# Attention: queries and placed row maxima summed in PSUM by TensorE, and copied out by ScalarE

## The chip, the cores and the metric

One core of one Trainium2 chip runs the whole program in one launch. The number that counts is the device time of that launch in microseconds (us), as the median of several runs. TensorE (PE; PEld is its weight load), VectorE (DVE), ScalarE (ACT), GpSimd (POOL) and the queues of DMA each run their own instructions in order and meet at semaphores.

## What is computed

Four sublayers follow one another on a residual x of 2 x 512 tokens by 512 channels: causal attention with 32 heads of 16, a gated feed-forward with low-rank side weights, a mixer, and a gated feed-forward with quantized weights. The change is inside the attention:

```
q = (x @ wq).reshape(b, s, H, HD); k = (x @ wk).reshape(b, s, H, HD); v = ...
q = _apply_rotary(q, cos, sin);    k = _apply_rotary(k, cos, sin)
scores = jnp.einsum('bqhd,bkhd->bhqk', q, k) * scale
scores = jnp.where(causal[None, None], scores, jnp.finfo(scores.dtype).min)
probs = jax.nn.softmax(scores, axis=-1)
out = jnp.einsum('bhqk,bkhd->bqhd', probs, v).reshape(b, s, d) @ wo
```

## The kernel before

The attention handles 32 pairs of heads (a pair of heads of one batch entry; `PAIRS`). Queries and keys of a pair stand in `q_stack(g)` and `k_stack(g)`, parts of `xt_hi` and `xt_lo` of 128 partitions by 512 tokens: 64 partitions a head, three copies of 16 channels split into high and low parts, and two spare partitions for a row maximum. Each pair is done in two passes.

- ONE (four blocks i = 3, 2, 1, 0 of 128 queries): TensorE makes scores (L1264) and adds the causal mask with four small products (L1268); VectorE takes the negated row maxima (`negmax`, L916) and, after block 0, writes them as a high and a low part into `max_row` (L924, L925).
- PLACE: TensorE multiplies `max_row` by an identity, four products of 128 columns (L1294), so that the maxima land in bank 6 of PSUM on the two spare partitions, zeros elsewhere. VectorE adds `q_stack(g)` to it and writes the sum into `q_less_max(g)`, a part of `w_hi` (L929).
- TWO (four blocks): TensorE makes the transposed scores less their maxima from `k_stack` and `q_less_max` (L1302), ScalarE takes the exponential into `probs` (L743), GpSimd zeroes the upper triangle of the diagonal block (L649).
- PV (per two pairs, four blocks): probabilities by values, into bank 7 (L1313). ScalarE copies bank 7 out after block 3 (`heads_t`, L749), FLIP turns it on TensorE (L1287) and VectorE divides by the sums (L937, L938).
- TURN (every fourth pair): TensorE turns a block of queries and keys (L1222), ScalarE copies it out as a high part (L737), VectorE subtracts for the low part (L913). The queue of SP writes both to `turned` in HBM, and GpSimd's queue loads the next stacks from there (STACK, L630).

One list, `PERIODS`, sets the order for all engines; each engine picks its own entries from it and runs them in that order. A period handles TWO of pairs a and b, and ONE of the next two:

```
(TWO a 0) (ONE next_a 3) (TURN) (PLACE b) (TWO a 1) (ONE next_a 2) (PV m-1, 3) (TWO b 0) (ONE next_a 1) (TWO b 1)
(ONE next_a 0) (PV m, 0) (TWO a 2) (ONE next_b 3) (FLIP) (PV m, 1) (TWO b 2) (ONE next_b 2) (PLACE next_a) (TWO a 3)
(ONE next_b 1) (PV m, 2) (TWO b 3) (ONE next_b 0)
```

m counts the periods from 0 to 15, after an opening one (m = -1). TURN stands in the opening one and in m = 0, 2, 4, 6, 8, 10. ONE, TWO, TURN and FLIP share a ring of three pairs of PSUM banks in the order of the list: an entry of TensorE waits (`ring_free`) until the third one before it has been read. So in a period without TURN the first product of TWO b waits for the maxima of ONE next_a 3, in one with TURN for the low part of TURN (L913). Besides, TWO i = 0 of a pair waits for its `q_less_max`.

Of the kernel before, what the change touches and what calls it, by code (L numbers as in the profile page):

```python
# [14 lines left out]
F32 = mybir.dt.float32  # L15
# [3 lines left out]
ALU = mybir.AluOpType  # L19
# [3 lines left out]
P = 128  # L23
# [24 lines left out]
def sandwich(nc, a, out):  # L48
# [3 lines left out]
    def sem(name):  # L52
        if name not in sems:
            sems[name] = es.enter_context(nc.semaphore(name))
        return sems[name]
# [4 lines left out]
    with es:  # L60
# [640 lines left out]
        def _(act):  # L701
# [28 lines left out]
            for e in PERIODS:  # L730
                what, g, i = e
                if what == TURN:

                    act.wait_ge(sem("block_psum"), g + 1)
                    if g >= 3:
                        act.wait_ge(sem(f"turned_out{g % 2}"), 12 * 16 * (g // 2))
                    nc.scalar.activation(turned_hi(g), pair_of_banks(e), ACT.Copy).then_inc(sem("block_hi"), 1)  # L737
                elif what == TWO:
                    act.wait_ge(sem("scores_t"), nth[e] + 1)
                    if nth[e] >= PROBS:  # L740
                        _, g0, i0 = TWOS[nth[e] - PROBS]
                        act.wait_ge(sem("pv"), TB * (g0 // 2) + i0 + 1)
                    nc.scalar.activation(probs[:, nth[e] % PROBS, :, 0:(TB - i) * P], pair_of_banks(e)[:, :, 0:(TB - i) * P],  # L743
                                         ACT.Exp).then_inc(sem("exp"), 1)
                elif what == PV and i == TB - 1:
                    act.wait_ge(sem("pv"), TB * (g + 1))
                    if g >= 2:
                        act.wait_ge(sem("flipped"), g - 1)
                    nc.scalar.activation(heads_t[:, g % 2, :], bank[7][:, :], ACT.Copy).then_inc(sem("heads_t"), 1)  # L749
# [92 lines left out]
        def _(dve):  # L842
# [66 lines left out]
            for e in PERIODS:  # L909
                what, g, i = e  # L910
                if what == TURN:
                    dve.wait_ge(sem("block_hi"), g + 1)
                    nc.vector.tensor_tensor(turned_lo(g), pair_of_banks(e), turned_hi(g).bitcast(F32), ALU.subtract).then_inc(sem("block_split"), 1)  # L913
                elif what == ONE:
                    dve.wait_ge(sem("scores"), nth[e] + 1)
                    nc.vector.tensor_reduce(negmax[:, g, i, :], pair_of_banks(e)[:, :, 0:(i + 1) * P], AX_X, ALU.max,  # L916
                                            negate=True).then_inc(sem("row_max"), 1)
                    if i == 0:

                        dve.wait_ge(sem("row_max"), TB * (g + 1))  # L920
                        if g:
                            dve.wait_ge(sem("placed"), g)
                        rows = max_row[:, :, :].rearrange("p i (h r) -> p i h r", h=2)
                        link(nc.vector.tensor_copy(rows[:, :, :, 3 * HD], negmax[:, g, :, :]))  # L924
                        nc.vector.tensor_tensor(rows[:, :, :, 3 * HD + 1], negmax[:, g, :, :], rows[:, :, :, 3 * HD].bitcast(F32),  # L925
                                                ALU.subtract).then_inc(sem("max_row"), 1)
                elif what == PLACE:
                    dve.wait_ge(sem("placed"), g + 1)
                    nc.vector.tensor_tensor(q_less_max(g), bank[6][:, :], q_stack(g).bitcast(F32), ALU.add).then_inc(sem("q_less_max"), 1)  # L929
                elif what == FLIP:  # L930

                    b, n = divmod(g, NPAIR // 2)
                    dve.wait_ge(sem("flipped"), g + 1)
                    if b:
                        dve.wait_ge(sem("wo_split"), KD)
                    src = pair_of_banks(e)[:, 0, :].rearrange("p (i h r) -> p i h r", i=TB, h=4)
                    link(nc.vector.reciprocal(einv[:, g, :, :], src[:, :, :, HD]))  # L937
                    nc.vector.tensor_tensor(y[:, TB * b:TB * b + TB, 4 * HD * n:4 * HD * (n + 1)].rearrange("p i (h d) -> p i h d", h=4),  # L938
                                            src[:, :, :, 0:HD], einv[:, g, :, :].unsqueeze(3).to_broadcast([P, TB, 4, HD]),
                                            ALU.mult).then_inc(sem("o_ready"), 1)  # L940
# [260 lines left out]
        def _(pe):  # L1201
# [70 lines left out]
            for e in PERIODS:  # L1272
# [10 lines left out]
                elif what == FLIP:  # L1283
                    ring_free(e)
                    pe.wait_ge(sem("heads_t"), g + 1)
                    for t in range(TB):
                        ins = nc.tensor.transpose(pair_of_banks(e)[:, 0, t * P:(t + 1) * P], heads_t[:, g % 2, t * P:(t + 1) * P], ident[:, :])  # L1287
                    ins.then_inc(sem("flipped"), 1)
                elif what == PLACE:
                    pe.wait_ge(sem("max_row"), g + 1)  # L1290
                    if g:
                        pe.wait_ge(sem("q_less_max"), g)
                    for t in range(TB):
                        ins = nc.tensor.matmul(bank[6][:, t * P:(t + 1) * P], max_row[:, t, :], ident_r[:, :], start=True, stop=True)  # L1294
                    ins.then_inc(sem("placed"), 1)
                elif what == TWO:
                    ring_free(e)
                    if i == 0:
                        pe.wait_ge(sem("q_less_max"), g + 1)
                    for h in range(2):  # L1300
                        rows = slice(64 * h, 64 * h + 64)
                        ins = nc.tensor.matmul(pair_of_banks(e)[:, h, 0:(TB - i) * P], k_stack(g)[rows, i * P:(i + 1) * P],  # L1302
                                               q_less_max(g)[rows, i * P:S], start=True, stop=True)
                    ins.then_inc(sem("scores_t"), 1)
                elif what == PV:
                    pe.wait_ge(sem("probs"), nth[TWO, 2 * g + 1, i] + 1)
                    if i == 0 and g:
                        pe.wait_ge(sem("heads_t"), g)
                    for four in range(4):
                        pair, h = 2 * g + four // 2, four % 2  # L1310
                        b, p = PAIRS[pair]
                        col = (2 * p + h) * (HD + 1)
                        ins = nc.tensor.matmul(bank[7][32 * four:32 * four + 32, i * P:S], v[:, TB * b + i, col:col + 32],  # L1313
                                               probs[:, nth[TWO, pair, i] % PROBS, h, 0:(TB - i) * P], start=(i == 0), stop=(i == TB - 1))
                    ins.then_inc(sem("pv"), 1)
# [252 lines left out]
```

## Time and profile before

| what | value |
|---|---|
| runs | 897.25, 898.45, 899.44 us, median 898.45 |
| profiled execution | 898.1 us, of which the span is 896.0 |
| busy in the span | PE 770.9, DVE 557.7, POOL 433.4, ACT 316.8 us |
| attention with its pairs | about 107 to 326 us of the span: PE 188.0 of 219.0, DVE 152.16, ACT 103.01, POOL 67.31 |
| granted TensorE clock there | 0.87 of full, mean |

A granted clock of 1.00 is 2.4 GHz, 0.50 is 1.2 GHz; values between are means of stretches that hold both. The engines of the attention work one after another on each pair and in parallel on different pairs, so the busy shares alone don't say what one instruction is worth: that is read from the place where it stands in a period, and from what waits for it.

### The profile page before, as it was taken

How to read it: one execution, taken by the hardware profiler on the slowest of the kernel's cores; microseconds unless marked ns; L12 is line 12 of the kernel's file. 1: busy time of each engine (PE TensorE's matmuls, PEld its weight loads, DVE VectorE, ACT ScalarE, POOL GpSimd, SP SyncE). 2: the span in 40 equal slices, each digit the busy share in tenths (PEclk: the TensorE clock that was granted, in tenths of full speed). 3: DMA queues.
4: the chain of work that ended last, by engine and by line, in shares of the span. 5: the costliest groups of instructions: out<-in, count | busy, mean ns of one | idle time of the engine just before them, and what ended most of it. 6: DMA issues, size and time to landing. Idle time of an engine off the chain costs nothing.

```text
span 896.0 us, 12432 instructions
## 1 busy us (share of the span) xinstructions
PE 770.9 (86%) x4387; PEld 559.8 (62%) x4387; DVE 557.7 (62%) x1130; ACT 316.8 (35%) x504; POOL 433.4 (48%) x545
## 2 busy tenths in 40 slices
PE   4799487988899878868998889899699999779995
PEld 3578344544545446646886767777487777568884
DVE  5443276776778719997546686886967555760015
ACT  3111034445545535522422433323253333233420
POOL 3233113432323317455645675657576575556632
PEclk9899768898989979979999999999799999889998
DMA  8100573244442040145585343445233231133201
GB/s 296 48 0 1 165 218 104 101 144 165 165 166 95 1 155 4 52 143 189 194 267 187 121 122 117 145 134 168 74 103 97 68 86 48 47 95 105 77 10 47
DMA packets 56941, 101.34 MB, mean 113 GB/s; under 512 B 13616, under 2 KB 17200, under 8 KB 54704
## 3 DMA queue, kind: packets, MB, share of 16 engines
q1 hardware_dynamic: 54576, 83.78, 29.2%
q0 software_dynamic: 2304, 16.78, 5.5%
q8 instruction: 35, 0.57, 0.3%
q14 instruction: 26, 0.21, 0.1%
HBM read 74.58 MB, written 27.00 MB: 113 GB/s over the span
## 4 chain that ended last, share of the span: by engine, by line
PE 54%; DVE 27%; POOL 5%; issue 5%; ACT 4%; DMA 3%; SPq 1%; DVEq 0%; ACTq 0%; POOLq 0%
PE psum L1392 18%; PE psum L1412 11%; PE psum L1215 7%; PE psum L1313 4%; DVE negmax L916 4%; PE psum L1302 3%; DVE bnst L984 2%; DVE w_hi L929 2%; ACT probs L743 2%; DMA xt_lo<-turned 2%; PE psum L1264 2%; PE psum L1448 2%; DVE stage_w L1076 1%; DVE hn L1153 1%; PE psum L1287 1%
## 5 line engine op out<-in xcount | busy, mean ns | idle before, releaser
L1392 PE MATMUL psum<-xt_hi,wgu_hi 128*128 128x512 f32 (+1 forms) x352 | 144.4, 410 | 7.8 <-issue 7.8
L673 POOL TENSOR_TENSOR wgu_lo<-raw,wgu_hi 128x512 fp32r<-128x512 f32 (+1 forms) x88 | 118.5, 1353 | 60.1 <-ACT wgu_hi L803 60.0
L1392 PE MATMUL psum<-xt_hi,wgu_lo 128*128 128x512 f32 (+1 forms) x352 | 143.0, 406 | 0.0
L1392 PE MATMUL psum<-xt_lo,wgu_hi 128*128 128x512 f32 (+1 forms) x352 | 142.2, 404 | 0.0
L916 DVE TENSOR_REDUCE negmax<-psum 128x2 f32<-128x1024 f32 (+3 forms) x128 | 104.9, 822 | 54.4 <-PE psum L1268 52.2
L649 POOL TENSOR_SCALAR_AFFINE_SELECT probs<-probs 128x256 f32<-128x256 f32 x128 | 52.3, 409 | 154.9 <-ACT probs L743 154.7
L743 ACT ACTIVATE probs<-psum 128x1024 f32<-128x1024 f32 (+3 forms) x128 | 88.4, 704 | 107.2 <-PE psum L1302 106.2
L1055 DVE TENSOR_TENSOR hf<-sg,psum 128x512 f32<-128x512 f32 (+1 forms) x44 | 30.1, 684 | 100.7 <-PE psum L1392 71.6
L1392 PEld LDWEIGHTS psum<-xt_hi,wgu_hi 128*128 128x128 f32 (+1 forms) x352 | 67.3, 191 | 24.7 <-issue 9.6
L673 POOL TENSOR_TENSOR wd_lo<-raw,wd_hi 128x512 fp32r<-128x512 f32 (+1 forms) x44 | 59.8, 1370 | 39.9 <-ACT wd_hi L810 39.8
L1412 PE MATMUL psum<-wd_hi,h_hi 128*128 128x512 f32 (+1 forms) x176 | 73.3, 416 | 6.7 <-DVE y L1064 3.9
L678 POOL TENSOR_TENSOR h_lo<-hf,h_hi 128x512 fp32r<-128x512 f32 (+1 forms) x44 | 61.1, 1388 | 35.5 <-ACT h_hi L824 35.5
L1392 PEld LDWEIGHTS psum<-xt_hi,wgu_lo 128*128 128x128 f32 (+1 forms) x352 | 67.1, 190 | 17.1 <-issue 0.7
L1392 PEld LDWEIGHTS psum<-xt_lo,wgu_hi 128*128 128x128 f32 (+1 forms) x352 | 67.3, 191 | 16.5 <-issue 0.7
L803 ACT ACTIVATE wgu_hi<-raw 128x512 fp32r<-128x512 f32 (+1 forms) x88 | 53.6, 618 | 61.7 <-PE psum L1392 31.2
L1412 PE MATMUL psum<-wd_hi,h_lo 128*128 128x512 f32 (+1 forms) x176 | 70.8, 402 | 0.0
L1412 PE MATMUL psum<-wd_lo,h_hi 128*128 128x512 f32 (+1 forms) x176 | 70.8, 402 | 0.0
L1302 PE MATMUL psum<-w_hi,xt_lo 64*128 64x512 f32 (+3 forms) x256 | 56.0, 434 | 15.1 <-DVE w_hi L929 12.9
L1302 PEld LDWEIGHTS psum<-w_hi,xt_lo 64*128 64x128 f32 x256 | 25.8, 196 | 64.2 <-issue 36.5
L1264 PE MATMUL psum<-xt_lo,xt_hi 64*128 64x512 f32 (+3 forms) x256 | 48.4, 370 | 19.5 <-DMA xt_lo<-turned 12.7
L1313 PE MATMUL psum<-probs,v 128*32 128x128 f32 (+3 forms) x512 | 57.2, 523 | 4.2 <-POOL probs L649 3.7
L817 ACT ACTIVATE sg<-psum 128x512 f32<-128x512 f32 (+1 forms) x44 | 26.3, 598 | 67.6 <-PE psum L1392 38.3
(193 smaller groups left out, 1482.3 us busy)
## 6 DMA issues: line engine op xcount, KB each, us to landing
raw<-full SPq DMA_DIRECT2D x60, 256.0 KB, 2.7
raw<-in_gu_t SPq DMA_DIRECT2D x40, 256.0 KB, 3.6
xt_hi<-turned POOLq DMA_DIRECT2D x8, 1024.0 KB, 5.2
xt_lo<-turned POOLq DMA_DIRECT2D x8, 1024.0 KB, 8.4
stage_w<-in_w SPq DMA_DIRECT2D x30, 256.0 KB, 3.2
full<-stage_w SPq DMA_DIRECT2D x30, 256.0 KB, 2.0
turned<-w_hi SPq DMA_DIRECT2D x56, 128.0 KB, 5.1
turned<-w_lo SPq DMA_DIRECT2D x28, 128.0 KB, 3.4
```

The source lines that it names most:

```text
L649: nc.gpsimd.affine_select(out=diagonal, in_=diagonal, pattern=[[0, 2], [1, P]], compare_op=ALU.is_ge, fill=0.0, base=0, channel_multiplier ...
L673: nc.gpsimd.tensor_tensor(lo, src, hi.bitcast(F32), ALU.subtract).then_inc(sem("w_lo"), 1)
L678: nc.gpsimd.tensor_tensor(h_lo[0:n, r % RING, :], hf[0:n, r % 2, :], h_hi[0:n, r % RING, :].bitcast(F32), ALU.subtract).then_inc(sem("h_lo ...
L743: nc.scalar.activation(probs[:, nth[e] % PROBS, :, 0:(TB - i) * P], pair_of_banks(e)[:, :, 0:(TB - i) * P], ACT.Exp).then_inc(sem("exp"), 1)
L803: nc.scalar.activation(wgu_hi[:, (2 * r + c) % 4, :, 0:n], src.rearrange("p (k h) -> p k h", k=KD)[:, :, 0:n], ACT.Copy).then_inc(sem("w_h ...
L916: nc.vector.tensor_reduce(negmax[:, g, i, :], pair_of_banks(e)[:, :, 0:(i + 1) * P], AX_X, ALU.max, negate=True).then_inc(sem("row_max"), 1)
L1215: ins = nc.tensor.matmul(dst, lhs(i, k), rhs(j, k), start=start and n == 0, stop=stop and n == len(todo) - 1)
L1264: nc.tensor.matmul(dst[:, h, :], lhs[rows, :], rhs[rows, :], start=True, stop=False)
L1302: ins = nc.tensor.matmul(pair_of_banks(e)[:, h, 0:(TB - i) * P], k_stack(g)[rows, i * P:(i + 1) * P], q_less_max(g)[rows, i * P:S], start= ...
L1313: ins = nc.tensor.matmul(bank[7][32 * four:32 * four + 32, i * P:S], v[:, TB * b + i, col:col + 32], probs[:, nth[TWO, pair, i] % PROBS, h ...
L1392: ins = nc.tensor.matmul(bank[q % 3][0:n, :], (wgu_hi, wgu_lo)[hi_w][:, q % 4, k, 0:n], XT[hi_x][:, k, ch * 512:ch * 512 + 512], start=ite ...
L1412: ins = nc.tensor.matmul(bank[3 + j % 2][:, :], (h_hi, h_lo)[lo_h][0:n, r % RING, j * P:(j + 1) * P], (wd_hi, wd_lo)[lo_w][0:n, r % RING, ...
```

## The change

PLACE gets a product ahead of its four: the identity `ident_r` by `q_stack(g)`, 512 columns in one product, opens the sum in bank 6, and the four products of the maxima are added onto it. It stands behind the same two waits (for `max_row`, and for the bank's reader). What then stands in bank 6 is already the sum, and ScalarE copies it to `q_less_max(g)` at PLACE's place in its own order. VectorE's addition L929 is gone, 32 of 128x512. All semaphores and the list are as before.

```diff
@@ scalar
+                elif what == PLACE:
+                    act.wait_ge(sem("placed"), g + 1)
+                    nc.scalar.activation(q_less_max(g), bank[6][:, :], ACT.Copy).then_inc(sem("q_less_max"), 1)
@@ vector
-                elif what == PLACE:
-                    dve.wait_ge(sem("placed"), g + 1)
-                    nc.vector.tensor_tensor(q_less_max(g), bank[6][:, :], q_stack(g).bitcast(F32), ALU.add).then_inc(sem("q_less_max"), 1)
@@ tensor
                     pe.wait_ge(sem("max_row"), g + 1)
                     if g:
                         pe.wait_ge(sem("q_less_max"), g)
+                    nc.tensor.matmul(bank[6][:, :], ident_r[:, :], q_stack(g), start=True, stop=False)
                     for t in range(TB):
-                        ins = nc.tensor.matmul(bank[6][:, t * P:(t + 1) * P], max_row[:, t, :], ident_r[:, :], start=True, stop=True)
+                        ins = nc.tensor.matmul(bank[6][:, t * P:(t + 1) * P], max_row[:, t, :], ident_r[:, :], start=False, stop=t == TB - 1)
                     ins.then_inc(sem("placed"), 1)
```

ScalarE's order in a period with TURN, from the exponential of TWO a 0 to that of TWO b 0, before (L743 the exponentials, L737 TURN's copy, L749 `heads_t`):

```order
L743 ACTIVATE probs<-psum 128x1024
L737 ACTIVATE w_hi<-psum 128x1024
L743 ACTIVATE probs<-psum 128x2x384
L749 ACTIVATE heads_t<-psum 128x512
L743 ACTIVATE probs<-psum 128x1024
```

and after the change (L747 is the new copy, L752 is `heads_t`):

```order
L743 ACTIVATE probs<-psum 128x1024
L737 ACTIVATE w_hi<-psum 128x1024
L747 ACTIVATE w_hi<-psum 128x512
L743 ACTIVATE probs<-psum 128x2x384
L752 ACTIVATE heads_t<-psum 128x512
L743 ACTIVATE probs<-psum 128x1024
```

The copy stands behind TURN's copy and ahead of the exponential of TWO a 1, `heads_t` and the exponential of TWO b 0.

VectorE's order in the same place, before (L913 is TURN's low part, L929 the addition):

```order
L916 TENSOR_REDUCE negmax<-psum 128x2
L913 TENSOR_TENSOR w_lo<-psum,w_hi 128x1024
L929 TENSOR_TENSOR w_hi<-psum,xt_hi 128x512
L916 TENSOR_REDUCE negmax<-psum 128x2 x3
L924 CAST max_row<-negmax 128x8
```

and after (L919 is `negmax`, L916 TURN's low part):

```order
L919 TENSOR_REDUCE negmax<-psum 128x2
L916 TENSOR_TENSOR w_lo<-psum,w_hi 128x1024
L919 TENSOR_REDUCE negmax<-psum 128x2 x3
L927 CAST max_row<-negmax 128x8
L928 TENSOR_TENSOR max_row<-negmax,max_row 128x8
```

The maxima of ONE next_a 2 now follow TURN's low part directly.

TensorE's order around PLACE b in a period without TURN, before:

```order
L1268 MATMUL psum<-causal,ident 128x64 x2
L1294 MATMUL psum<-ident_r,max_row 128x128 x4
L1302 MATMUL psum<-w_hi,xt_lo 128x384 x2
L1264 MATMUL psum<-xt_lo,xt_hi 128x384 x2
L1268 MATMUL psum<-causal,ident 128x128 x2
```

and after:

```order
L1268 MATMUL psum<-causal,ident 128x64 x2
L1293 MATMUL psum<-xt_hi,ident_r 128x512
L1295 MATMUL psum<-ident_r,max_row 128x128 x4
L1303 MATMUL psum<-w_hi,xt_lo 128x384 x2
L1264 MATMUL psum<-xt_lo,xt_hi 128x384 x2
```

The product of 512 columns stands between the mask of ONE next_a 3 and the four products of the maxima; all that follows is in the old order.

## Rows read from the trace of the kernel before

**Rows 1.** Windows, a plain period: stretch, length, PE, PEld, DVE, ACT, POOL busy, clock, DMA.

```profile
269.65:280.52 10.87, 9.94 (x114) 5.59 (x112) 8.98 (x17) 6.03 (x10) 4.25 (x11) 1.00 0.04 8
```

**Rows 2.** Chain of waits in that period: start, us, what the chain ran through.

```profile
271.01 1.03 ACT probs L743
...
272.57 1.06 PE psum L1313 x8
...
277.25 0.60 DVE w_hi L929
...
278.50 0.50 PE psum L1302 x2
```

**Rows 3.** Timeline of PE and ACT in that period: start, us, instruction, idle before it.

```profile
268.52 0.66 PE L1294 MATMUL psum<-ident_r,max_row 128*128 128x128 f32 x4
...
278.15 0.26 PE L1268 MATMUL psum<-causal,ident 64*128 64x128 bf16 x4
...
268.18 1.03 ACT L743 ACTIVATE probs<-psum 128x1024 f32<-128x1024 f32 x1 [0.42 <-PE psum L1302]
269.60 0.81 ACT L743 ACTIVATE probs<-psum 128x768 f32<-128x768 f32 x1 [0.40 <-PE psum L1302]
270.31 0.60 ACT L749 ACTIVATE heads_t<-psum 128x512 f32<-128x512 f32 x1
```

**Rows 4.** Timeline of PE, ACT and DVE behind TURN in period m = 10.

```profile
255.17 0.43 PE L1313 MATMUL psum<-probs,v 128*32 128x128 f32 x8
257.26 0.57 PE L1302 MATMUL psum<-w_hi,xt_lo 64*128 64x512 f32 x2 [1.67 <-DVE w_hi L929]
...
254.24 1.03 ACT L737 ACTIVATE w_hi<-psum 128x1024 fp32r<-128x1024 f32 x1 [0.33 <-PE psum L1222]
255.16 0.81 ACT L743 ACTIVATE probs<-psum 128x768 f32<-128x768 f32 x1
255.85 0.60 ACT L749 ACTIVATE heads_t<-psum 128x512 f32<-128x512 f32 x1
...
255.29 1.23 DVE L913 TENSOR_TENSOR w_lo<-psum,w_hi 128x1024 fp32r<-128x1024 f32 x1 [0.85 <-ACT w_hi L737]
256.44 0.68 DVE L929 TENSOR_TENSOR w_hi<-psum,xt_hi 128x512 fp32r<-128x512 f32 x1
```

**Rows 5.** Windows, columns as in rows 1: behind two TURNs, and a stretch much later.

```profile
257.60:264.30 6.70, 6.48 (x44) 2.75 (x40) 3.48 (x8) 2.33 (x3) 1.23 (x3) 0.50 1.01 348
229.90:233.60 3.70, 1.62 (x24) 0.81 (x18) 3.38 (x4) 2.35 (x5) 0.41 (x1) 1.00 1.02 387
233.70:237.00 3.30, 3.30 (x20) 1.18 (x22) 0.78 (x3) 0.87 (x2) 0.78 (x2) 0.50 1.00 335
569.60:581.60 12.00, 8.99 (x43) 7.19 (x42) 11.76 (x25) 2.39 (x4) 8.36 (x9) 1.00 0.35 104
```

**Rows 6.** Windows, five stretches from TURN's L929 to the next PLACE b's: first, sum.

```profile
152.99:166.64 13.65, 12.21 (x100) 6.40 (x100) 8.94 (x17) 4.80 (x9) 4.68 (x10) 0.75 0.63 226
...
sum 64.82, PE 58.08 PEld 30.74 DVE 44.73 ACT 23.97 POOL 17.82; mean PE 11.62 PEld 6.15 DVE 8.95 ACT 4.79 POOL 3.56
```

**Rows 7.** Timeline of PE, products of 512 columns of the same types, back to back.

```profile
330.39 0.63 PE L1215 MATMUL psum<-w_lo,o_hi 128*128 128x512 f32 x1
330.82 0.63 PE L1215 MATMUL psum<-w_hi,o_lo 128*128 128x512 f32 x1
...
332.82 0.39 PE L1215 MATMUL psum<-w_lo,o_hi 128*128 128x512 f32 x1
333.05 0.40 PE L1215 MATMUL psum<-w_hi,o_lo 128*128 128x512 f32 x1
```

**Rows 8.** Groups by line: line, engine, operation, count, busy us, mean ns, idle before.

```profile
L757 ACT ACTIVATE o_hi<-psum 128x512 fp32r<-128x512 f32 x8 | 4.8, 595 | 3.0 <-PE psum L1325 3.0
```

**Rows 9.** Chain of waits in period m = 0, up to the next stacks' load.

```profile
122.84 0.61 DVE w_hi L929
...
126.12 10.04 DMA xt_lo<-turned
```

## The prediction

> **What bounds the kernel now.** I read the windows first, to see how full the engines are in one period of the attention, then the chain of waits through that period, then the timelines at the two places where a PLACE stands, and last the windows again for the granted clock.
>
> A period without TURN (a plain one) takes 10.87 us, with TensorE busy 9.94, VectorE 8.98, ScalarE 6.03, at a clock of 1.00 [rows 1]. TensorE is nearly the bound, and the chain changes hands: from 272.57, where PV begins, it runs through TensorE, at the end through VectorE's maxima with the addition L929 (0.60) among them, and reaches the next period's first product at 278.50 [rows 2]. But TensorE's own last instruction ends at 278.15 + 0.26 = 278.41 [rows 3]: VectorE is late there by 0.09 us only. In the first part of the period the chain goes through the exponential of TWO b 0 at 271.01 [rows 2].
>
> A period with TURN has another place. TensorE runs dry at 255.17 + 0.43 = 255.60 and starts TWO b 0 only at 257.26, on L929, which had to queue behind TURN's low part on VectorE (255.29 + 1.23 = 256.52) [rows 4]. And behind this gap the clock falls: 0.50 from 257.60 to 264.30, with TensorE busy 6.48 of 6.70; behind the TURN before it, TensorE is busy 1.62 of 3.70 and then runs at 0.50 from 233.70 to 237.00 [rows 5]. The five stretches from a TURN's L929 to the next PLACE b take 64.82 us together [rows 6], where five plain ones at 10.87 would take 54.35. So the slow clock behind the five TURNs of m = 2 to 10 costs 64.82 - 54.35 = 10.47 us, more than all the additions' places on the chain.
>
> **The change, part by part.** Removed: 32 additions on VectorE. Added: 32 products of 512 columns and 32 copies on ScalarE. Nothing shows these two, so they are priced by the nearest rows. The product: the same types and shape follow one another every 333.05 - 332.82 = 0.23 us at full clock, and every 0.43 (330.39 to 330.82) at half [rows 7]. I take 0.23, since PLACE ran at full clock in the plain period; 0.43 is the upper end, and zero the lower, where TensorE waits anyway. The copy: 0.595 us for 128x512 out of PSUM into the same type [rows 8]; on ScalarE the next instruction starts some 0.1 before its end (269.60 + 0.81 = 270.41, the next at 270.31) [rows 3], so it takes 0.50 to 0.60 of the queue.
>
> The Trainium skill ("TensorE: Matmul & The Clock Gate", Back-to-back issue gap) gives 131 ns for a 512-column product in a sustained stream. The rows say 0.23 at full clock, so they decide; by the page's figure the 22 products counted below as on the path would cost about 2.2 us less, an estimate of 885.7 in place of the forecast.
>
> Late half of a plain period, from PV at 272.57 to the next one's start, 5.93 us: VectorE's part shrinks by 0.60, and TensorE, late by only 0.09, becomes the bound with 0.23 more. Cost 0.23 - 0.09 = +0.14. ScalarE is idle there, so the copy of PLACE next_a is covered.
>
> Early half: TensorE now ends the last mask of the previous period just as the new one starts, so the maxima of ONE next_b 0, and `max_row` with them, come about 0.1 later. PLACE moves from 268.52 to 268.62 and ends 0.66 + 0.23 later, at 269.51; the copy runs from there. Queued behind it on ScalarE stand the exponential of TWO a 1 (from 269.60 to about 270.03), `heads_t` (270.31 to 270.74) and the exponential of TWO b 0, 0.50 behind that, at 271.24 where it was at 271.01 [rows 2, 3]. GpSimd's mask and PV wait for it: +0.23. A plain period therefore becomes 0.14 + 0.23 = +0.37 us longer.
>
> Period with TURN: the ring lets TWO b 0 start when TURN's low part is read, 256.52, and 0.14 later (the lag that L929 shows: its end 257.12, the product 257.26) [rows 4]. That is 256.66 for 257.26: -0.60. The copy is covered here: behind TURN's copy from about 255.17 to 255.77, with the exponential of TWO a 1 at 255.67, `heads_t` at 256.38, and ScalarE free for TWO b 0 at 256.88, when that product is still running (0.57 long). With +0.14 in the late half: -0.46.
>
> Sum without the clock, over periods: five pairs of one with TURN and one plain (m = 2 to 11), 5 x (-0.46 + 0.37) = -0.45; m = 12 to 14, 3 x 0.37 = +1.1; the last, +0.23; m = 0, whose L929 is on the chain that ends in the load of the next stacks [rows 9], -0.60 (its late half is hidden under that load, 10.04 us long); m = 1, which begins on the load, between 0 and +0.37, taken as 0. In all +0.3: nothing.
>
> The clock: TensorE's gap behind TURN shrinks at both ends, from 1.66 us to 1.66 - 0.60 - 0.23 = 0.83. The stretch of 3.70 that preceded a fall had 3.70 - 1.62 = 2.08 idle; it would have 1.25. Plain periods, idle 10.87 - 9.94 = 0.93 in all, never lose the clock; 569.60 to 581.60, idle 3.01 of 12.00, kept 1.00 as well [rows 1, 5]. So the ends are: the falls stay (0) or all five go (-10.47). 1.25 is nearer to 0.93 than to 2.08, and I take the second: 898.1 + 0.3 - 10.5 = 887.9, on the profiled execution of 898.1 (span 896.0 and 2.1 around it), which stands 0.35 below the median. I forecast 888.0, where one or two falls may remain (1.4 to 2.8 each by the stretches of [rows 6]), so 884.5 to 892.
>
> What is late next behind TURN is its own low part on VectorE, then the exponential of TWO b 0. The loads of stacks are issued a period ahead of their use; a period with TURN at full clock would still take about 12.4 us (10.87, plus 2.0 to 2.1 for TURN, less 0.5), above the slowest load, 10.04 [rows 9].
>
> **The rivals.**
>
> *The gap shrinks, but the clock falls as before.* 0.83 us of idle remains in every TURN, and the waits for the exponential of TWO b 0 follow it. Then only the sum without the clock is left: 898.4, with all steps between this and the forecast possible. For it: the idle of 1.25 lies between what kept and what lost the clock; against it, that all five lost it at 1.66 and no plain period does. The Trainium skill ("TensorE: Matmul & The Clock Gate", A second HAM failure mode) says that micro-idles between groups of products, through cycling of PSUM, make the clock swing and cost throughput between bursts; the gap of 1.66 agrees, and whether 0.83 is still such an idle no run here shows.
>
> *TensorE pays the product in full.* If its weights aren't loaded under the products before it, or the clock is low where it stands, it costs 0.43 in the 22 places counted above (two in each of eight plain periods, one in five TURN periods, one in the last): 22 x 0.20 = +4.4, and with the falls kept 902.8, slower. It decides from 0.23 + (900.25 - 898.4)/22 = 0.31 us on, if the clock gains nothing. Against it: the back-to-back rows at 0.23 include a load of new weights each.
>
> *The addition's removal is real, but the next stacks become late.* The attention would gain only until the loads bind, at most about 2 us a period with TURN given back: around 893 to 897. The slack of two us above speaks against it.
>
> The Trainium skill ("ScalarE: Activation LUTs", Rules for kernel authors) tells to put additions and the like on VectorE, not on ScalarE. Here ScalarE only copies, and the rows have that at 0.595 us against 0.68 for the addition on VectorE, so the rule's reason doesn't hold for this size and type; by the rule the removed term would be no gain at all, which is the second rival's side.
>
> **How the numbers follow.** Forecast (884.5 to 892): 0.58. Clock as before, 892 to 900.25: 0.20, a third of it below 896.65. Late stacks, 893 to 897: 0.06. Product in full, above 900.25: 0.12. Better than 884.5, since other falls go too: 0.04. A measurement of this kernel can tell about 0.2%, 1.8 us, from no change: faster is below 896.65, slower above 900.25. Faster: 0.58 + 0.07 + 0.06 + 0.04 = 0.75, less 0.02 for late stacks near the bound: 0.73. Same: 0.14. Slower: 0.13. The range from 884.0 to 899.0 leaves out the last two cases.
>
> **What would show it.** Right: the gap of PE ahead of TWO b 0 behind TURN is 0.8 to 0.9 and ends on TURN's low part; the clock there stays 1.00; stretches from TURN to the next PLACE b take about 11.2; plain periods take 11.1 to 11.3 with TWO b 0's exponential behind `heads_t`; the new copy takes 0.6 and the new product 0.23. Wrong: the clock falls behind TURN with the gap at 0.83 (first rival), products that follow the new one by 0.4 (second), or PE waiting for `xt_lo<-turned` in L1264 beyond the opening periods (third).

## The result, and the profile after

The changed kernel takes 893.42 us (median of 4 runs, 892.46 to 893.71) against 898.68 for the kernel before in the same comparison (897.25 to 899.44): ratio 0.9941, 95% interval 0.9924 to 0.9959. It is faster, by 5.3 us; 888.0 was forecast from 898.45, a gain of about 10.5. The time lies in the stated range (884.0 to 899.0); the gain is half of what was said. A later comparison gave 0.9943 (0.9915 to 0.997), with single runs of the changed kernel from 888.73 to 898.99 us, against 897.63 to 901.45 and one 904.10 for the kernel before. This spread turns out to be part of the answer. One run of a later kernel, early_product, took 1225.94 us at a mean granted clock of 0.56, and is left out of its time below.

The profiled execution after took 892.46 us, span 890.4. First the page's busy times, then the two new instructions in the groups by line (line, engine, operation, count, busy us, mean ns, idle before and its releaser):

```profile
PE 769.0 (86%) x4419; PEld 562.5 (63%) x4419; DVE 538.1 (60%) x1098; ACT 331.5 (37%) x536; POOL 433.9 (49%) x545
...
L747 ACT ACTIVATE w_hi<-psum 128x512 fp32r<-128x512 f32 x32 | 19.1, 596 | 22.4 <-PE psum L1295 22.4
L1293 PE MATMUL psum<-xt_hi,ident_r 128*128 128x512 f32 x32 | 16.7, 523 | 1.7 <-DVE max_row L928 0.7
```

The copy takes 0.596 us, as [rows 8] had it. A product's listed duration (0.523) is longer than the distance to the next one (271.31 to 271.65 below); what the new product costs is therefore read from the distance to what follows PLACE. The timeline of PE and ACT at PLACE b of a plain period after, and the product that followed PLACE before (L1302):

```profile
271.31 0.50 PE L1293 MATMUL psum<-xt_hi,ident_r 128*128 128x512 f32 x1
271.65 0.56 PE L1295 MATMUL psum<-ident_r,max_row 128*128 128x128 f32 x4
272.14 0.45 PE L1303 MATMUL psum<-w_hi,xt_lo 64*128 64x384 f32 x2
```

```profile
269.12 0.44 PE L1302 MATMUL psum<-w_hi,xt_lo 64*128 64x384 f32 x2
```

```profile
272.24 0.60 ACT L747 ACTIVATE w_hi<-psum 128x512 fp32r<-128x512 f32 x1 [0.54 <-PE psum L1295]
272.74 0.80 ACT L743 ACTIVATE probs<-psum 128x768 f32<-128x768 f32 x1
273.43 0.60 ACT L752 ACTIVATE heads_t<-psum 128x512 f32<-128x512 f32 x1
273.91 1.04 ACT L743 ACTIVATE probs<-psum 128x1024 f32<-128x1024 f32 x1
```

PLACE takes 272.14 - 271.31 = 0.83 of TensorE's time where it took 269.12 - 268.52 = 0.60 [rows 3]: 0.23 more. On ScalarE the copy pushes the exponential of TWO a 1, `heads_t` and the exponential of TWO b 0 ahead of itself in an unbroken row, 0.50, 0.69 and 0.48 apart.

Behind TURN (timeline of PE, ACT and DVE, m = 8), the counterpart of [rows 4]:

```profile
226.13 0.42 PE L1314 MATMUL psum<-probs,v 128*32 128x128 f32 x8
227.29 0.50 PE L1303 MATMUL psum<-w_hi,xt_lo 64*128 64x512 f32 x2 [0.73 <-DVE w_lo L916]
...
225.87 0.59 ACT L747 ACTIVATE w_hi<-psum 128x512 fp32r<-128x512 f32 x1
226.35 0.82 ACT L743 ACTIVATE probs<-psum 128x768 f32<-128x768 f32 x1
227.04 0.62 ACT L752 ACTIVATE heads_t<-psum 128x512 f32<-128x512 f32 x1
227.83 1.73 ACT L743 ACTIVATE probs<-psum 128x1024 f32<-128x1024 f32 x2 [0.17 <-PE psum L1303]
...
226.01 1.23 DVE L916 TENSOR_TENSOR w_lo<-psum,w_hi 128x1024 fp32r<-128x1024 f32 x1 [0.85 <-ACT w_hi L737]
```

The gap is 227.29 - 226.55 = 0.74 and ends on TURN's low part, not on an addition. The windows (columns as in [rows 1]), from one copy of TURN to the next, the first and the last of four, and a plain period:

```profile
154.01:177.66 23.65, 21.58 (x229) 12.56 (x228) 17.01 (x30) 14.80 (x24) 11.25 (x23) 1.00 0.46 157
...
224.95:248.60 23.65, 21.59 (x229) 12.59 (x228) 17.00 (x30) 14.80 (x24) 7.65 (x19) 1.00 0.47 157
272.24:283.46 11.22, 10.40 (x112) 5.90 (x112) 7.97 (x15) 6.89 (x11) 3.62 (x9) 1.00 0.51 189
```

In this execution the clock holds behind all five TURNs. A pair of periods takes 23.65 us; before, its four pairs took 26.64, 25.29, 26.28 and 25.24 (the starts of TURN's copies L737 in the timeline: 150.79, 177.43, 202.72, 229.00, 254.24).

So where is the rest? Cut by three marks that every execution has, the first product of ONE (L1264) behind the first stacks' load, and the starts of TURN's copies of m = 2 and m = 10, the spans divide like this (us):

| execution | its time | to the first ONE | to TURN m = 2 | m = 2 to 10 | to the end |
|---|---|---|---|---|---|
| before | 898.1 | 106.99 | 43.80 | 103.45 | 641.80 |
| after | 892.46 | 108.24 | 45.77 | 94.59 | 641.80 |
| forecast of the difference | -10.2 | 0 | -0.6 | -8.5 | -1.1 |
| measured difference | -5.64 | +1.25 | +1.97 | -8.86 | 0.00 |

(The forecast's parts: -0.6 for m = 0; four of the slow stretches, 8.1, and four pairs at -0.09; then the fifth stretch of 2.3, the fifth pair, and +1.3 for the last plain periods.) The middle came as forecast. The opening lost 2 us, the end gave nothing, and the first column is work that the change doesn't touch. The last column holds 569 us behind the attention that the change doesn't touch either: up to ScalarE's first copy behind the attention (`o_hi<-psum`, 327.14 before, 321.27 after) it gained 72.90 - 72.67 = 0.23, and lost as much behind it.

In the opening the second stacks' load is waited for. Timeline of PE and windows after, the wait with its end and what follows:

```profile
132.74 0.48 PE L1303 MATMUL psum<-w_hi,xt_lo 64*128 64x512 f32 x2
136.71 0.80 PE L1264 MATMUL psum<-xt_lo,xt_hi 64*128 64x512 f32 x2 [3.49 <-DMA xt_lo<-turned]
...
136.70:141.60 4.90, 4.89 (x31) 3.13 (x31) 2.18 (x2) 2.00 (x3) 0.41 (x1) 0.50 0.01 3
141.60:149.40 7.80, 7.56 (x46) 3.20 (x44) 3.28 (x7) 2.32 (x4) 3.06 (x5) 0.50 0.00 0
```

and the same place before:

```profile
136.30 0.50 PE L1264 MATMUL psum<-xt_lo,xt_hi 64*128 64x512 f32 x2 [2.25 <-DMA xt_lo<-turned]
...
136.30:138.10 1.80, 1.80 (x22) 1.29 (x23) 1.17 (x2) 0.20 (x1) 0.00 (x0) 1.00 0.01 3
138.10:144.90 6.80, 6.39 (x47) 3.02 (x44) 3.39 (x8) 3.54 (x5) 1.58 (x4) 0.50 0.00 0
```

After, TensorE waits 3.49 us for the load, and period m = 1 runs at 0.50 from its first product to 149.40; before it waited 2.25, and 6.80 us of that period were slow. At the far end, the last period (windows, from about the last PLACE to the turning of the outputs, after, then before):

```profile
305.00:320.00 15.00, 9.55 (x67) 4.28 (x67) 1.30 (x4) 6.24 (x11) 3.22 (x8) 0.77 0.00 0
```

```profile
311.90:326.00 14.10, 8.60 (x67) 3.77 (x67) 2.07 (x6) 6.12 (x10) 3.22 (x8) 0.87 0.01 2
```

TensorE is idle for over a third of it in both, at a lower clock after.

### The profile page after: what moved, and what is told of

Read it like the earlier page. It is cut to its first block, busy times and chain, and to the rows that moved or that the text cites. A ratio compares the mean times of both kernels' runs of the same rounds, so it can differ in the third digit from the quotient of the medians.

```text
span 890.4 us, 12496 instructions
## 1 busy us (share of the span) xinstructions
PE 769.0 (86%) x4419; PEld 562.5 (63%) x4419; DVE 538.1 (60%) x1098; ACT 331.5 (37%) x536; POOL 433.9 (49%) x545
## 4 chain that ended last, share of the span: by engine, by line
PE 57%; DVE 22%; POOL 6%; issue 5%; ACT 5%; DMA 3%; SPq 1%; DVEq 0%; ACTq 0%; POOLq 0%
PE psum L1393 19%; PE psum L1413 10%; PE psum L1215 7%; PE psum L1314 4%; PE psum L1303 3%; DVE bnst L984 3%; ACT probs L743 3%; DMA xt_lo<-turned 2%; PE psum L1264 2%; PE psum L1449 2%; DVE stage_w L1076 1%; PE psum L1293 1%; DVE x L997 1%; PE psum L1287 1%; POOL wd_lo L673 1%
## 5 line engine op out<-in xcount | busy, mean ns | idle before, releaser
L919 DVE TENSOR_REDUCE negmax<-psum 128x2 f32<-128x1024 f32 (+3 forms) x128 | 104.8, 824 | 62.7 <-PE psum L1268 61.0
L743 ACT ACTIVATE probs<-psum 128x1024 f32<-128x1024 f32 (+3 forms) x128 | 88.4, 707 | 60.9 <-PE psum L1303 58.6
L1264 PE MATMUL psum<-xt_lo,xt_hi 64*128 64x512 f32 (+3 forms) x256 | 48.5, 375 | 23.1 <-DMA xt_lo<-turned 14.0
L1303 PE MATMUL psum<-w_hi,xt_lo 64*128 64x512 f32 (+3 forms) x256 | 53.9, 420 | 5.5 <-DVE w_lo L916 4.5
L1314 PE MATMUL psum<-probs,v 128*32 128x128 f32 (+3 forms) x512 | 51.4, 476 | 4.5 <-POOL probs L649 3.9
```

What stands on the lines that cost most here:

```text
L1264: nc.tensor.matmul(dst[:, h, :], lhs[rows, :], rhs[rows, :], start=True, stop=False)
```

## The experiments

Theory A, formed from these rows: the gain behind TURN is the clock's, and part of it is lost to the clock again in the opening. Theory B: the long opening is an accident of that execution, or the new product and copy lengthen it themselves. Theory C came with the spread of the runs: the shorter gap behind TURN still costs the clock, in some executions.

### after_again: the change, unaltered

> The changed kernel unaltered, to see whether its opening repeats. Theory A (the time saved in period m = 0 only lengthens TensorE's wait for the second load of stacks, 2.25 us before and 3.49 after, the clock falls to 0.50 before the load lands and stays there through most of period m = 1): 893 to 894 us, with a granted clock of 0.50 from about the landing of that load for 10 us or more, and full clock behind every later TURN. Theory B (the long slow stretch was an accident of one execution, and the rest of the missing gain is ahead of the attention): the slow stretch of m = 1 is no longer than the 6.8 us of the kernel before.

Measured: 894.57 us (10 runs, 888.73 to 898.99), ratio 0.9943 (0.9915 to 0.997). Its profiled execution (894.8) has 110.06, 44.44, 95.96 and 642.29 in the columns of the table: the opening is long in part only, and one pair behind a TURN took 25.01. Period m = 1 is slow for 10.2 us (138.1 to 148.3), as theory A said, but one TURN lost the clock. So the opening varies, and so does the middle. Neither theory alone explains the spread of 10 us.

### before_look2, after_look2, after_look3: more executions of both

No edit. One more profiled execution of the kernel before, two more of the changed one.

> The kernel before, a second profiled execution, to see which parts of it differ from one execution to the next. If the long gap of 1.66 us behind TURN costs the clock wherever it falls in time: the four distances between successive TURNs of m = 2 to 10 are again 25.2 to 26.7 us each, and the stretch from the second stacks' load to the TURN of m = 2 is 13 to 16. If the falls depend on when the gap comes: some of the distances near 23.8.

> The changed kernel, another profiled execution. Its runs spread from 888.7 to 899.0 us, those of the kernel before from 897.6 to 901.5 with one at 904.1. Theory C (the shorter gap behind TURN costs the clock in some executions and not in others, by when it comes): in an execution near 898 several distances between TURNs are 25 or more, in one near 889 to 894 all are 23.65. Theory A alone (only the opening and the last periods vary): all four at 23.65 whatever the time.

> As after_look2, one more profiled execution. Theory C: the time and the number of distances between TURNs over 24 us go together, about 1.4 to 3 us for each. Theory A alone: the distances are 23.65 each, and the time goes with the stretch from the second stacks' load to the TURN of m = 2.

Measured: 900.21, 891.71 and 898.33 us. Windows from one TURN's copy to the next, before_look2 (first two), then after_look3 (all four):

```profile
153.13:179.58 26.45, 23.47 (x227) 12.82 (x225) 19.13 (x34) 12.95 (x20) 11.18 (x23) 0.87 0.42 141
179.58:204.77 25.19, 22.04 (x227) 12.33 (x225) 19.15 (x34) 12.94 (x19) 9.52 (x21) 0.93 0.43 146
```

```profile
154.89:181.36 26.47, 24.46 (x229) 13.61 (x228) 16.95 (x30) 14.79 (x24) 11.24 (x23) 0.87 0.41 141
181.36:206.55 25.19, 23.12 (x229) 13.13 (x228) 17.00 (x30) 14.79 (x24) 9.46 (x21) 0.93 0.43 147
206.55:230.17 23.62, 21.57 (x229) 12.58 (x228) 17.00 (x30) 14.79 (x23) 7.63 (x19) 1.00 0.46 156
230.17:253.81 23.64, 21.58 (x229) 12.59 (x228) 17.00 (x30) 14.79 (x24) 7.61 (x19) 1.00 0.47 157
```

The kernel before loses the clock behind every TURN, in both executions. The changed one holds it behind two of these four here, and in the other three executions behind four, three and three. The two pairs with a fall take as long as before, 26.47 and 25.19; the fall costs them 1.6 to 2.8 us. That execution lost the clock once more, behind the fifth TURN (0.50 from 257.70 to 261.10), and is the slowest of the four. That is theory C, though not in every detail: the fastest execution, after_look2, also lost the clock behind one TURN (a pair of 25.01), where C expected none. All executions side by side:

| execution | its time | to the first ONE | to TURN m = 2 | m = 2 to 10 | to the end |
|---|---|---|---|---|---|
| before_look2 | 900.21 | 108.61 | 44.52 | 103.07 | 641.95 |
| after_look2 | 891.71 | 107.58 | 44.11 | 95.91 | 642.04 |
| after_look3 | 898.33 | 110.48 | 44.41 | 98.92 | 642.46 |
| mean of before (2) | 899.2 | 107.80 | 44.16 | 103.26 | 641.9 |
| mean of after (4) | 894.3 | 109.09 | 44.68 | 96.35 | 642.1 |

The middle gains 6.9 us on the mean where 8.5 was forecast, the opening costs 0.5 where 0.6 was to be gained, the end 0.2 where 1.1 was to be gained. The first column reaches from 106.99 to 110.48 over these six executions, ahead of any edit; it moves the time by up to 3.5 us and says nothing of the change. So the falls are only part of the spread: of the 6.6 us between after_look2 and after_look3, 3.0 lie in the middle and 2.9 in the first column. And the opening's 0.5 is no more than two executions of one kernel differ by; its two parts, at the load below, are clearer.

### old_opening: the first pairs the old way

Pairs 0 to 3 have no further product, and VectorE adds; the others go the new way. Shortened to its conditions, on ScalarE, VectorE and TensorE, against the kernel before:

```diff
+                elif what == PLACE and (g >= 4):
...
+                elif what == PLACE and not (g >= 4):
...
+                    summed = g >= 4
+                    if summed:
+                        nc.tensor.matmul(bank[6][:, :], ident_r[:, :], q_stack(g), start=True, stop=False)
```

> The changed kernel, but pairs 0 to 3 (the opening, m = 0 and PLACE b of m = 1) have the old way: no further product, VectorE adds. Theory A: the wait for the second load is 2.2 to 2.3 us as before, the slow stretch of m = 1 about 6.8 us, and the whole 1 to 2 us shorter than the changed kernel, 891 to 892.5. If the missing gain lies elsewhere: 893 to 894.

Measured: 893.81 us (8 runs), ratio 0.9938 (0.9915 to 0.9961): no better than the change. The wait for the load in the waits of PE (engine, line waited for, us in all, times, longest):

```profile
PE psum L1267 <- DMA xt_lo<-turned: 2.6, 1, 2.6
```

It is shorter than after the change (3.49), yet to TURN m = 2 it took 45.59 us, as long as in the profiled execution after. So theory A falls in its detail: a slow stretch of 10.2 us in m = 1 comes with a wait of 2.6 us too, and in before_look2 with the old code throughout and a wait of 2.13. What the wait costs varies from one execution to the next.

### fill_load: work in the wait for the load

```diff
+                    if g == 4 and i == TB - 1:
+                        pe.wait_ge(sem("q_less_max"), 3)
+                        for _ in range(13):
+                            nc.tensor.matmul(bank[6][:, :], ident_r[:, :], q_stack(0), start=True, stop=True)
                     if i == TB - 1:
                         pe.wait_ge(sem(f"stack_in{g // 4 % 2}"), 32 * (g // 8 + 1))
```

> The changed kernel with 13 further products of 512 columns into bank 6 (their result is not used), issued just before TensorE waits for the second load of stacks: about 3.0 us of work at full clock in a gap of 3.49. Theory A (the idle wait costs the clock in period m = 1): the clock stays at 1.00 through m = 1, the stretch from the landing of the load to the next TURN falls from 16.2 us to about 12 to 13, and the whole to about 890. Theory B (the new product and copy lengthen m = 1 by themselves): that stretch stays near 16 and the whole at 893 to 894.

Measured: 889.74 us (4 runs, 887.71 to 892.19), ratio 0.9891 (0.9864 to 0.9918). The timeline of PE at the wait, and the window behind it:

```profile
133.62 3.30 PE L1282 MATMUL psum<-xt_hi,ident_r 128*128 128x512 f32 x13
136.84 0.51 PE L1264 MATMUL psum<-xt_lo,xt_hi 64*128 64x512 f32 x2
...
136.80:149.60 12.80, 12.10 (x127) 7.33 (x127) 9.03 (x15) 6.94 (x12) 5.89 (x12) 1.00 0.01 2
```

The load lands no earlier, at 135.64, and the products even outlast it by 1.2 us; but the clock is 1.00 all through m = 1, and the opening takes 42.26 us in place of 44.1 to 45.8. Products whose result nobody reads shorten the kernel: the idle wait costs the clock, and that costs the opening 1.9 to 3.5 us. The part of theory B that blames the new product and copy is out, since both are here too. Its other part holds for the size alone: the 13.7 us at half clock in the first execution after are the longest of four. At the load the executions compare like this (us; the landing is that of `xt_lo<-turned`, L630, counted from the first ONE):

| execution | wait for the load | it lands | from there to TURN m = 2 | half clock about m = 1 |
|---|---|---|---|---|
| before | 2.25 | 29.17 | 14.63 | 6.8 |
| before_look2 | 2.13 | 29.06 | 15.46 | 10.2 |
| after | 3.49 | 28.33 | 17.43 | 13.7 |
| after_again | 3.28 | 28.24 | 16.19 | 10.2 |
| after_look2 | 3.19 | 28.06 | 16.05 | 10.2 |
| after_look3 | 3.54 | 28.41 | 16.00 | 10.2 |
| old_opening | 2.64 | 29.41 | 16.18 | 10.2 |
| fill_load | filled | 28.35 | 13.91 | 0 |

So the change brings the load forward by 0.86 us on the mean, somewhat more than the 0.6 that was forecast, and loses 1.4 behind it, which the filling gives back.

### before_fill: the old kernel with a shorter gap behind TURN

```diff
+                    for _ in range(4 if g in (5, 9, 13, 17, 21) else 0):
+                        nc.tensor.matmul(bank[6][:, :], ident_r[:, :], q_stack(g), start=True, stop=True)
                     for t in range(TB):
                         ins = nc.tensor.matmul(bank[6][:, t * P:(t + 1) * P], max_row[:, t, :], ident_r[:, :], start=True, stop=True)
```

> The kernel before, with four products of 512 columns put ahead of PLACE b in the five periods with TURN from m = 2 to 10 (their result is overwritten). VectorE still adds. TensorE's gap behind TURN then shrinks from 1.66 to about 0.75 us, and the first product of TWO b 0 still waits for L929. If the slow clock behind TURN comes from that gap: the clock stays at 1.00 there, stretches from TURN to the next PLACE b of about 10.9 in place of 12.3 to 13.7, and the whole at 887 to 890. If the falls come from something else in a period with TURN, or only VectorE's release of TWO b 0 matters: 898 to 900.

Measured: 892.76 us (5 runs, 887.34 to 897.58), ratio 0.991 (0.9878 to 0.9941). Timeline of PE behind the TURN of m = 8, and windows from TURN to TURN (first and third) of the execution of 897.58:

```profile
228.98 1.17 PE L1294 MATMUL psum<-xt_hi,ident_r 128*128 128x512 f32 x4
...
232.29 0.50 PE L1304 MATMUL psum<-w_hi,xt_lo 64*128 64x512 f32 x2 [0.73 <-DVE w_hi L929]
...
153.46:180.14 26.68, 24.49 (x229) 13.71 (x228) 19.13 (x34) 13.06 (x20) 11.24 (x23) 0.87 0.40 140
...
205.45:229.26 23.81, 21.53 (x229) 12.70 (x228) 19.20 (x34) 13.06 (x19) 7.67 (x19) 1.00 0.46 156
```

The gap is 0.73, as long as after the change, and still ends on VectorE's addition: nothing is taken off VectorE. The expected 887 to 890 was missed, since the clock was expected to hold behind every TURN: in this execution two of the first four pairs fell, two held at 23.81, and the fifth TURN held too. But the kernel is as fast as the changed one, and as spread. The gain of the change is thus bought by the shorter gap, and can be had by idle work alone; the time that L929 itself took from the chain is paid back in the plain periods (turn_only_filled below).

### both_fills: the change with both gaps filled

```diff
+                    for _ in range(3 if g in (5, 9, 13, 17, 21) else 0):
+                        nc.tensor.matmul(bank[6][:, :], ident_r[:, :], q_stack(g), start=True, stop=True)
```

with the 13 products of fill_load.

> The changed kernel with 13 products ahead of the wait for the second load (as fill_load) and 3 more products of 512 columns ahead of PLACE b in the five periods with TURN, so that TensorE's gap there is about 0.15 us in place of 0.83. Theory C (in some executions the gap of 0.83 still costs the clock): no slow clock behind any TURN in any execution, the runs draw together, spread below 5 us, median 886.5 to 889. Theory A alone: no better than fill_load, 889 to 890.

Measured: 889.22 us (4 runs, 887.99 to 890.38), ratio 0.9881 (0.9855 to 0.9907). TensorE's gap behind TURN is 0.05, the pairs take 23.76 to 23.78, and the clock never falls between m = 1 and m = 11. The runs lie within 2.4 us, but there are only four, and the median is where theory A alone had it, no better than that of fill_load beyond the intervals. So the time of this kernel doesn't tell A from C; the windows of after_look3 do.

### vector_copy: the sum in PSUM, copied by VectorE

```diff
                 elif what == PLACE:
                     dve.wait_ge(sem("placed"), g + 1)
-                    nc.vector.tensor_tensor(q_less_max(g), bank[6][:, :], q_stack(g).bitcast(F32), ALU.add).then_inc(sem("q_less_max"), 1)
+                    nc.vector.tensor_copy(q_less_max(g), bank[6][:, :]).then_inc(sem("q_less_max"), 1)
```

with the product on TensorE as in the change.

> The product half of the change alone: queries and maxima are summed in PSUM by the further product, but VectorE copies the sum out, at the addition's place. If what gains is that TWO b 0 behind TURN no longer queues behind VectorE: the gap there stays about 1.4 us and ends on VectorE's copy, the clock falls in most periods with TURN, distances between TURNs 25 or more, and the whole 900 to 904, slower than before by the product on TensorE. If the sum in PSUM by itself helps (less work per element on VectorE): 893 to 898.

Measured: 899.7 us (10 runs), ratio 1.0007 (0.9986 to 1.0027): no gain, and not the loss that was expected. Timeline, PE and DVE behind the TURN of m = 8:

```profile
231.95 0.50 PE L1303 MATMUL psum<-w_hi,xt_lo 64*128 64x512 f32 x2 [1.43 <-DVE w_hi L929]
...
231.13 0.68 DVE L929 CAST w_hi<-psum 128x512 fp32r<-128x512 f32 x1
```

The copy on VectorE takes as long as the addition did (0.68), so TWO b 0 waits as before, and only the product has shortened the gap, from 1.66 to 1.43. Even that let two of four pairs (24.24 and 24.21) keep the clock; the other two took 27.00 and 25.65, and the fifth TURN lost it. The four pairs together gained 2 us (101.10 against 103.45 and 103.07 before), and the part from there to the first copy behind the attention lost 1.5 of it (74.42 against 72.90). The sum in PSUM is worth nothing by itself; of the gap's shortening from 1.66 to 0.74 the copy's place on ScalarE makes 0.69.

### turn_only_filled: the new way behind TURN only

The copy on ScalarE and the addition on VectorE go by the same rule (shortened; against the kernel before):

```diff
+                    summed = g in (5, 9, 13, 17, 21)
+                    for _ in range(3 if summed else 0):
+                        nc.tensor.matmul(bank[6][:, :], ident_r[:, :], q_stack(g), start=True, stop=True)
```

with the 13 products of fill_load.

> Only PLACE b of the five periods with TURN from m = 2 to 10 goes the new way (sum in PSUM, copy by ScalarE); the other 27 PLACEs go the old way, added by VectorE. The two fillings are kept: 13 products ahead of the second load, 3 ahead of PLACE b behind TURN (results not used). If the new way costs a plain period its 0.35 us (10.87 before, 11.22 in the trace after) and gains only behind TURN: plain periods at 10.87 again, distance between TURNs about 23.2 to 23.3 in place of 23.65, whole 884.5 to 887. If taking the work off VectorE helps everywhere and plain periods were longer for another reason: 889 or more.

Measured: 885.66 us (4 runs, 883.96 to 887.33), ratio 0.9837 (0.9806 to 0.9868): the lowest median of all, and faster than both given kernels. A window from TURN to TURN, and two additions of VectorE at PLACE b of successive plain periods:

```profile
222.41:245.67 23.26, 21.64 (x229) 12.73 (x228) 18.60 (x33) 13.45 (x21) 7.65 (x19) 1.00 0.48 160
...
269.05 0.68 DVE L932 TENSOR_TENSOR w_hi<-psum,xt_hi 128x512 fp32r<-128x512 f32 x1
279.91 0.68 DVE L932 TENSOR_TENSOR w_hi<-psum,xt_hi 128x512 fp32r<-128x512 f32 x1
```

Plain periods are back at 10.86 us, and pairs take 23.24 to 23.34. So the change loses 0.36 in every plain period and gains in those with TURN, as the sum had it.

### early_product: the product ahead of the wait for the maxima

```diff
-                    pe.wait_ge(sem("max_row"), g + 1)
                     if g:
                         pe.wait_ge(sem("q_less_max"), g)
...
                     nc.tensor.matmul(bank[6][:, :], ident_r[:, :], q_stack(g), start=True, stop=False)
+                    pe.wait_ge(sem("max_row"), g + 1)
```

on both_fills; the three filling products behind TURN (where the dots stand) move ahead of the wait with it.

> As both_fills, with the product of the queries issued ahead of the wait for max_row in place of behind it, so that TensorE does it while it waits for the maxima. If the plain period's 0.35 us comes from that product standing in the way from max_row to the copy and to the exponential of TWO b 0: plain periods about 11.0 in place of 11.22 and the whole 1 to 2 us shorter than both_fills, 887 to 888.5. If it comes from ScalarE's copy ahead of the exponentials: no difference from both_fills, 889.

Measured: 887.2 us (median of three runs, 887.20 to 888.34), ratio 0.9858 (0.9825 to 0.9892), where both_fills had 0.9881 (0.9855 to 0.9907). The direction is the expected one, but the intervals overlap, and no profile of it is compared here, so the length of its plain periods isn't known. Left open.

## Why the prediction was right and wrong

- **The terms without the clock were right in their sum, one of them by luck.** The gap behind TURN was to be 0.83 and end on TURN's low part: 0.74, and it does; the product follows the low part's end by 0.05 (227.24 to 227.29), where 0.14 was taken. A pair without falls takes 23.81 in before_fill, where VectorE still adds; with -0.09 that is 23.72, and 23.65 was measured. From a TURN's PLACE b to the next one 11.5 us pass where about 11.2 was expected. The copy was priced at 0.595: 0.596. A plain period was to cost +0.37 and cost +0.35 (11.22 against 10.87 [rows 1]), but its halves came out otherwise. Timeline of PE, the first product of a plain period and PV in it, then the next period's first product, after, and the period's first product before:

```profile
270.16 0.47 PE L1303 MATMUL psum<-w_hi,xt_lo 64*128 64x512 f32 x2
...
275.48 1.06 PE L1314 MATMUL psum<-probs,v 128*32 128x512 f32 x8
...
281.28 0.26 PE L1268 MATMUL psum<-causal,ident 64*128 64x128 bf16 x4
281.38 0.47 PE L1303 MATMUL psum<-w_hi,xt_lo 64*128 64x512 f32 x2
```

```profile
267.63 0.50 PE L1302 MATMUL psum<-w_hi,xt_lo 64*128 64x512 f32 x2
```

  The late half costs nothing where +0.14 was said (275.48 to 281.38 is 5.90, against 5.93), and the early half +0.38 where +0.23 was said (270.16 to 275.48 is 5.32; 267.63 to 272.57 [rows 2] is 4.94). The prediction took the listed end of the last mask, 278.41, for the time when TensorE was free. But after the change the next product starts 0.10 behind the start of that mask; before, 0.35 had passed (278.15 to 278.50 [rows 2, 3]). So VectorE was late by 0.25 and not by 0.09, and that covers the product's 0.23. The early half then pays: from the period's first product to PLACE it takes 1.15 (270.16 to 271.31) against 0.89 (267.63 to 268.52). The two misses cancel.
- **The clock's term was mis-sized; this is the step that failed.** "I take the second", all five falls go, -10.47, with the clock as it was everywhere else. Behind the TURNs all five went in one profiled execution of four; in the others one, one and three of the five stayed, and the four pairs between m = 2 and 10 gained 6.9 on the mean in place of 8.5. The two ends (no fall goes, all go) were right, and the truth lies between them from one execution to the next; the range allowed for one or two falls, the forecast itself took none. [rows 5] already showed that the idle time of a stretch doesn't decide alone: 3.01 of 12.00 kept the clock, 2.08 of 3.70 lost it. The first rival (0.20) was not an alternative to the forecast but a share of the executions.
- **"In all +0.3: nothing" left out that the clock is lost elsewhere too,** which is the larger part of the same miss. The sum counted falls behind TURN only and took the opening and the last period as they stood. In m = 0 the change saves more than the 0.6 that was said: TensorE starts its last product ahead of the wait for the load 24.5 to 24.6 us behind the first ONE, where it took 26.56. But the load lands only 0.86 earlier, since it takes as long as before (9.8 to 10.1; 10.04 [rows 9]), and the rest becomes idle time. m = 1 was put at 0 to +0.37, and costs 1.4 more from the landing on. So the opening cost 0.5 on the mean instead of giving 0.6. From the TURN of m = 10 to the first copy behind the attention it takes 72.3 to 73.3 us, 72.84 on the mean, against 72.90 in both executions before: 0.1 gained instead of 1.1. The 6.8 us at half clock behind the fifth TURN were to go there; but half clock in this part, 11.6 us in both executions before, is still 8.1, 7.1, 11.5 and 8.0. Together these two parts miss by 2.1 us, the middle by 1.6.
- **The rest of the miss isn't the change's.** On the mean of the profiled executions the first column is 1.3 us longer after, and the work behind the attention 0.3.
- **The second rival, the product in full,** did not come: 0.23 at the place where it was read. **The third, late stacks,** neither: no wait for a load shows beyond the opening.
- **The base.** The profiled execution of before (898.1) was one of its faster ones: 898.68, 899.3, 899.96 and 899.73 were the medians of its runs in four comparisons. Against 899.3 the forecast of 888.0 was a gain of 11; measured are about 5.

What stays open: what decides, in an execution, whether a gap of 0.7 to 0.8 us costs the clock; and why the last periods spend more time at half clock than before.

## What to carry to other kernels

Where a gap on TensorE is followed by half clock, the gap's price is the slow stretch behind it, and shortening the gap can pay more than the time of the gap itself; but then the gain is a matter of how often the clock falls, and one profiled execution of each kernel doesn't show that: look at several, and at the spread of the runs. When more time is saved ahead of a wait than the awaited transfer gains, the rest turns into idle time, which here cost the clock again; filling the wait with products that nobody reads gained some 4 us. A sum that fits can hide two misreadings: compare each half, and on TensorE the starts of products, not their listed ends. And a step moved to a less busy engine is moved into that engine's order: the copy that was free behind TURN stood in front of the exponentials in every other period, so the best version moved it only where it paid.

## What had not been expected of the hardware

The same code, with the same gap of 0.74 us on TensorE, ran on at 1.00 or fell to 0.50 for 3.4 to 6.8 us, from one period to the next (after_look3: 26.47, 25.19, 23.62, 23.64 us for the same work). How often it fell went with the gap's length, over the five TURNs of m = 2 to 10 in each profiled execution: with 1.66 us behind 10 of 10, with 1.43 (vector_copy) behind 3 of 5, with 0.73 to 0.75 behind 7 of 35 (the changed kernel 5 of 20, before_fill 2 of 5, old_opening and fill_load 0 of 10), and with 0.05 (both_fills, turn_only_filled) behind 0 of 10. The kernel whose gaps lie in between had ten runs spread over 10 us (888.7 to 899.0); the one that always falls had most of 18 runs within 4 (897.6 to 901.5, one of 904.1), and those with both gaps filled four runs each within 2.4 and 3.4. Part of such a spread lies ahead of any edit, as the first column shows.
